# Pair products of a DLRM tower: two samples a product in 64-column strips of the PE array

## The reference

```python
e = jnp.stack([tbl_0[ids[:, 0]], ..., tbl_26[ids[:, 26]]], axis=1)   # [2048, 27, 128]
interactions = jnp.einsum('bfd,bgd->bfg', e, e)                     # a 27 x 27 gram per sample
x = interactions.reshape(B, 27 * 27)[:, TRIL_IDX]                   # 351 pairs
h = jnp.concatenate([bottom, x, bottom], axis=1)                    # 607 columns
h = jnp.maximum(h @ W_top1 + b_top1, 0.0)                           # 512
h = jnp.maximum(h @ W_top2 + b_top2, 0.0)                           # 256
y = h @ W_top3                                                      # 1
```

## Time and profile before

| | us |
|---|---|
| median of 3 runs | 420.68 |
| lowest, highest | 418.67, 421.84 |
| the profiled execution's own time | 419.41 |
| its span, first to last instruction | 417.6 |
| around the span | 1.8 |

### The profile page before, as it was taken

The page is one execution under the profiler, slowest core; times in us unless marked ns, Lnnn a source line. Parts: engine busy times, 40 slices in busy tenths (PEclk is TensorE's granted clock), DMA queues, the critical chain, the costliest instruction groups (busy, mean ns, idle before and its releaser), DMA issues.

```text
span 417.6 us, 8875 instructions
## 1 busy us (share of the span) xinstructions
PE 378.1 (91%) x3158; PEld 363.0 (87%) x3158; DVE 203.1 (49%) x493; ACT 157.4 (38%) x305; POOL 288.1 (69%) x279
## 2 busy tenths in 40 slices
PE   0457899959999989999899999999999999999987
PEld 0446789959999988999799998999999998999976
DVE  4587337924259124753349234744268235824140
ACT  2243342434332543235332453235423542335343
POOL 6777778777777778777777777777777777750000
PEclk9998999988999999999999999999999999999999
DMA  7999943557245661544324771645334652540000
GB/s 116 243 231 225 261 116 103 95 95 125 67 107 90 107 138 43 124 96 98 122 80 113 99 142 44 135 88 113 104 102 97 103 132 51 138 84 2 2 2 0
DMA packets 49790, 44.19 MB, mean 106 GB/s; under 512 B 30309, under 2 KB 42093, under 8 KB 49767
## 3 DMA queue, kind: packets, MB, share of 16 engines
q1 hardware_dynamic: 39440, 24.26, 30.9%
q0 software_dynamic: 8704, 17.84, 16.5%
q10 hardware_dynamic: 1623, 1.79, 1.6%
HBM read 39.01 MB, written 4.85 MB: 105 GB/s over the span
## 4 chain that ended last, share of the span: by engine, by line
PE 71%; DMA 12%; POOL 8%; issue 4%; ACT 3%; DVE 1%; SPq 1%; ACTq 0%; POOLq 0%
PE ps_build L742 26%; PE ps_gram L775 18%; PE ps_dense L783 8%; POOL rows L400 8%; DMA rows<-tbl_dram,idx 7%; PE ps_dense L811 6%; DMA raw<-tbl_dram 5%; PE ps_gram L771 3%; PE ps_build L754 2%; PE ps_dense L819 2%; PE ps_gram L754 2%; PE ps_gram L783 1%; ACT embT L561 1%; PE ps_build L811 1%; DVE table L415 1%
## 5 line engine op out<-in xcount | busy, mean ns | idle before, releaser
L400 POOL DMA_INDIRECT rows<-tbl_dram,idx x272 | 287.4, 1056 | 84.4 <-issue 77.4
L742 PE MATMUL ps_build<-hot,table 125*128 125x256 f32 x1280 | 164.2, 288 | 26.0 <-DVE table L415 18.4
L742 PEld LDWEIGHTS ps_build<-hot,table 125*128 125x128 f32 x1280 | 158.2, 194 | 26.8 <-issue 21.4
L440 DVE TENSOR_SCALAR hot<-id_raw 125x512 fp32r<-125x512 f32 x320 | 120.4, 435 | 5.5 <-PE ps_build L742 4.1
L775 PEld LDWEIGHTS ps_gram<-embT 128*107 128x107 f32 x896 | 89.8, 177 | 6.5 <-issue 3.0
L454 DVE COPY gram<-ps_gram 107x416 f32<-107x416 f32 x56 | 32.9, 588 | 125.0 <-PE ps_gram L775 120.6
L775 PE MATMUL ps_gram<-embT 128*107 128x104 f32 x896 | 92.4, 262 | 1.4 <-ACT embT L561 0.8
L554 ACT COPY embT<-ps_build 128x512 f32<-128x512 f32 x40 | 32.1, 804 | 108.6 <-PE ps_build L742 102.3
L573 ACT COPY gram<-ps_gram 107x416 f32<-107x416 f32 x56 | 28.4, 506 | 52.5 <-PE ps_gram L775 49.9
L783 PE MATMUL ps_dense<-pairT,w1p 120*128 120x256 f32 (+1 forms) x252 | 34.8, 283 | 0.0
L783 PEld LDWEIGHTS ps_dense<-pairT,w1p 120*128 120x128 f32 (+1 forms) x252 | 32.2, 191 | 0.0
(11 more groups left out here) (60 smaller groups left out, 169.4 us busy)
## 6 DMA issues: line engine op xcount, KB each, us to landing
id_raw<-ids_onehot_dram SPq DMA_DIRECT2D x40, 256.0 KB, 5.9
gram_dram<-gram SPq DMA_DIRECT2D x56, 84.5 KB
raw<-tbl_dram SPq DMA_DIRECT2D x10, 448.0 KB
rows<-tbl_dram,idx POOLq DMA_INDIRECT x272
bot<-bottom_dram SPq DMA_DIRECT2D x8, 128.0 KB, 6.5
w1p_raw<-w_pairs_dram ACTq DMA_DIRECT2D x1, 720.0 KB
raw<-tbl_dram SPq DMA_DIRECT2D x10, 52.0 KB
w2s<-w_dram ACTq DMA_DIRECT2D x1, 512.0 KB
```

The costliest lines, as they stand in the source:

```text
L400: nc.gpsimd.indirect_dma_start(rows[:, t, s * D:(s + 1) * D], None, tables[f], bass.IndirectOffsetOnAxis(idx[:, 2 * i + t, f:f + 1], 0)).t ...
L440: last = nc.vector.tensor_scalar(hot[0:VP, a % HOT_SLOTS, v, 0:w, :], shifted, float(v0 + v), None, ALU.is_equal)
L742: last = nc.tensor.matmul(bank[:, q * HALF:(q + 1) * HALF], table[0:VP, units[n][q], bits, row:row + D], hot[0:VP, a % HOT_SLOTS, v, q, :] ...
```

## The change

A product takes two samples (`DUO`): 53 stationary columns by 52 moving ones. Consecutive products go to one of two 64-column strips of the array (`tile_position`), and so to partitions 0 to 52 or 64 to 116 of PSUM. A tile is 64 products (128 pairs of instructions), 16 products to a bank, and the four gram banks hold the whole tile; each is emptied by one copy of 117 partitions × 416 elements, DVE's for banks 0 and 2 and ACT's for banks 1 and 3. `gram` holds both tiles. In the last half each sample is a product of its own, 26 × 26, in four 32-column strips: 128 products (256 pairs) a tile, two banks, one copy of 122 × 416 each. `embT` is no longer padded. The three `pairs_low` and `pairs_high` go before the gram copies of tile 0, `make_hot` of the next half goes three after tile 0 and two after tile 1, and layers 2 and 3 of the half before go behind all grams of tile 1.

```diff
-    GB = 8
-    GU = TILE // GROUP // GB
-    GRAMS = 2 * GU
-    GC = GROUP * PG
     JT = TILE // GROUP
-    GM = GROUP * FEATURES - 1
+    DUO = GROUP // 2
+    STRIP = DUO * PAD
+    GB = JT // 4
+    GRAMS = 4
+    GM = STRIP + DUO * FEATURES - 1
+    EB = JT // 2
...
-        gram = in_arena("gram", [GM, GROUP, PG, JT], fp32, 0)
+        gram = in_arena("gram", [GM, 2, DUO, PG, JT], fp32, 0)
...
+        def gram_piece(t, b):
+
+            src = gram_banks[b][0:GM, 0:GB * DUO * PG].rearrange("p (g c) -> p c g", g=GB)
+            return gram[:, t].rearrange("p k n j -> p (k n) j")[:, :, b * GB:(b + 1) * GB], src
+
+        def end_piece(t, b):
+
+            src = gram_banks[2 * t + b][0:GR, 0:EB * PG].rearrange("p (g n) -> p n g", n=PG)
+            return gram_end[:, :, t * JT + b * EB:t * JT + (b + 1) * EB], src
...
                 for k in range(GROUP):
-                    src = gram[k * FEATURES:k * FEATURES + PG, k, :, :].rearrange("p n j -> p (n j)")
+                    row = k // DUO * STRIP + k % DUO * FEATURES
+                    src = gram[row:row + PG, t, k % DUO, :, :].rearrange("p n j -> p (n j)")
...
-            def empty_gram(i, t, u):
-                if u == 0 and t == 0 and not is_half(i, FIRST):
+            def empty_gram(i, t):
+                if t == 0 and not is_half(i, FIRST):
                     dve.wait_ge(gram_out, TILE_OUT * 2 * i)
-                if u == 0 and t == 1 and not is_half(i, LAST):
-                    dve.wait_ge(gram_out, TILE_OUT * (2 * i + 1))
-                dve.wait_ge(grammed[1 if is_half(i, LAST) else 0], GRAMS * i + t * GU + u + 1)
                 if is_half(i, LAST):
-                    nc.vector.tensor_copy(*gram_pieces(t, u, 0))
-                    nc.vector.tensor_copy(*gram_pieces(t, u, 1)).then_inc(gram_dve, 1)
+                    dve.wait_ge(grammed[0], GRAMS * LAST + t + 1)
+                    nc.vector.tensor_copy(*end_piece(t, 0)).then_inc(gram_dve, 1)
                 else:
-                    nc.vector.tensor_copy(*gram_bank(u, 0)).then_inc(gram_dve, 1)
+                    for n in range(2):
+                        dve.wait_ge(grammed[0], GRAMS * i + 2 * t + n + 1)
+                        nc.vector.tensor_copy(*gram_piece(t, 2 * n + 0)).then_inc(gram_dve, 1)
...
-                for u in range(GU):
-                    empty_gram(i, 0, u)
-                    if u < 3:
-                        pairs_low(i - 1, u)
-                if more:
-                    make_hot(i + 1, 0)
-                for u in range(GU):
-                    empty_gram(i, 1, u)
-                    if more:
-                        make_hot(i + 1, 1 + u)
-
-            nc.vector.memset(emb_flat[:, HALF * FEATURES:HALF * PAD], 0.0).then_inc(pad_set, 1)
+                for c in range(3):
+                    pairs_low(i - 1, c)
+                grams(i, more)
+
+            def grams(i, more=True):
+                for t in range(2):
+                    empty_gram(i, t)
+                    for a in ((0, 1, 2), (3, 4))[t] if more else ():
+                        make_hot(i + 1, a)
...
             def second_tile(i, dense=None):
-                for u in range(GU):
-                    empty_gram(i, 1, u)
-                    if dense is not None and u < M2:
-                        layer2(dense, u)
-                    if dense is not None and u == M2:
-                        layer3(dense)
+                empty_gram(i, 1)
+                if dense is not None:
+                    for m in range(M2):
+                        layer2(dense, m)
+                    layer3(dense)
...
+            def pair_products(i, t):
+                pe.wait_ge(emb_done, BUILDS * i + nth("tile", t, TQ - 1) + 1)
+                for b in range(4):
+                    if t == 1 and b % 2 == 0:
+                        pe.wait_ge(gram_dve, GRAMS * i + b // 2 + 1)
+                    if t == 1 and b % 2 == 1:
+                        pe.wait_ge(gram_act, GRAMS * i + b // 2 + 1)
+                    for g in range(GB):
+                        for q in range(2):
+                            at = t * TILE + (b * GB + g) * GROUP + q * DUO
+                            x = embT[:, at:at + DUO, :]
+                            last = nc.tensor.matmul(
+                                gram_banks[b][STRIP * q:STRIP * q + GM - STRIP, g * DUO * PG:(g + 1) * DUO * PG],
+                                x.rearrange("p k g -> p (k g)")[:, 0:GM - STRIP], x[:, :, 1:FEATURES],
+                                start=True, stop=True, tile_position=(0, STRIP * q))
+                    last.then_inc(grammed[b % 2], 1)
+
+            def end_products(t):
+                pe.wait_ge(emb_done, BUILDS * LAST + nth("tile", t, TQ - 1) + 1)
                 for b in range(2):
...
+                    for g in range(EB):
+                        for k in range(GROUP):
+                            x = embT[:, t * TILE + (b * EB + g) * GROUP + k, :]
+                            last = nc.tensor.matmul(gram_banks[2 * t + b][PAD * k:PAD * k + PG, g * PG:(g + 1) * PG],
+                                                    x[:, 0:PG], x[:, 1:FEATURES], start=True, stop=True,
+                                                    tile_position=(0, PAD * k))
                     last.then_inc(grammed[b], 1)
...
             def relayout():
 
-                pe.wait_ge(gram_dve, GRAMS * HALVES)
-                pe.wait_ge(gram_act, GRAMS * HALVES)
+                pe.wait_ge(gram_dve, GRAMS * LAST + 2)
+                pe.wait_ge(gram_act, GRAMS * LAST + 2)
```

More of the change, by code:

```diff
@@ L506, in _ @@
                     split_table(q)
-            for n in range(GRAMS):
-                empty_gram(FIRST, n // GU, n % GU)
-                if n >= GRAMS - HOT_SLOTS:
-                    make_hot(1, n - GRAMS + HOT_SLOTS)
+            grams(FIRST)
             half(1)
@@ L626, in first_tile @@
             def first_tile(i, dense=None):
[L627 to L630 removed]
+                if dense is not None:
+                    for c in range(3):
+                        pairs_high(dense, c)
+                empty_gram(i, 0)
             def second_rows(i, dense=None):
@@ L879, in _ @@
             features(FIRST)
-            pe.wait_ge(pad_set, 1)
             first_tile(FIRST)
```

85 lines of the change are left out of this document (25 added, 60 removed).

## The result

The changed kernel takes 402.07 us (median of 4 runs, 401.51 to 407.32) where the kernel before took 421.26 in the same comparison (4 runs, 418.67 to 422.03): a ratio of 0.9583, 95% interval 0.9492 to 0.9673. The profiled execution took 401.51 (span 399.7) against 419.41 of the kernel before: 17.9 us less. I had forecast 413.6 and a range from 404, so the change did about two and a half times what I gave it. The direction holds, and so does the gain of PE with the gathers as the bound behind it; the size doesn't.

What follows compares the result with a forecast made beforehand. PE was taken as the bound, POOL's gathers close behind. Gain 7 us within the gathers' room, then last tile −0.7 + 0.2 and layer 3 +0.37: −7.1 from 419.41 gives 412.3; with the median 1.27 higher, 413.6, range 404 to 438.

Steps and rivals of the forecast that it cites:

- The grams: Gram products of halves 0 to 6: 31 ns a pair with strips side by side, a tile 4.0 us, saving 2.0.
- Borders: Switches between whole-array work and strips, twice a tile: 0.1 us each, 0.2 a tile.
- Layer 3: Layers 2 and 3 now adjacent: PE waits for ACT's relu and loses 0.37 us in each of seven halves.
- PE's half: PE's work in an ordinary half, 45.85 us before: two tiles save 2.0 each, less borders and the relu wait.
- The copies: Gram copies, 4 instead of 8 a half per engine at DVE 588 and ACT 506 ns: no time gained.
- The last half: Gram tiles of 256 small pairs at 24 ns, nearer to serial: 6.1 us a tile, saving 0.7.
- The relayout: After the last half's layers: its first bank waits for ACT to read layer 3's result, 0.8 us as before.
- The room ahead of PE: PE trails the gathered rows by some 10 us at the end; 7 taken as the gain before the last half's second tile.
- The step that failed: Gathers on POOL: pace held at 1.056 us plus about 0.30 issue, capping PE's gain at some 10 us.
- serial strips: Rival for the grams: strips take turns, an ordinary tile costs 0.6 us more, 428 us in all; chance 0.27.
- the fixed time a pair: Rival for the grams: below a fixed time fewer columns don't help; at 57 ns a pair 449 us; chance 0.21.
- late landings: Rival for the gathers: strips overlap but rows land 11 us late in every half, gain under 3 us, 418; chance 0.10.

Runs made afterwards that it cites:

- experiment 7: Separate kernel without the reference's computation: five phases of 34 gathers beside idle DVE, gram copies, one-hot parts, both in turn, subtractions; no whole time given.
- experiments 4 and 5: First: changed kernel unaltered on a slow chip, 628.61 us. Second: changed kernel, only tile 0's rows gathered anew after the first half, 486.55 us.

## Why the prediction was wrong

The steps in their order, own times of the profiled executions:

- **The grams.** I took 31 ns a pair between 26 and 57; it is 3.29/128 = 25.7, the end for strips fully side by side. By that line nothing is lost to the float32 product being two pairs in a row in one strip. A tile saves 2.7 us, not 2.0.
- **Borders.** I took 0.1 us each. The first part of layer 1 behind strips takes 1.63 instead of 1.46 us, layer 2 3.65 where two parts took 3.50: 0.15 to 0.17 on leaving the strips, nothing visible on entering them. Right in sum, 0.2 a tile.
- **Layer 3.** I took 0.37 us of waiting for the relu. From 113.91 to 115.07 it is 1.16 us where layer 3 took 0.95: 0.2.
- **PE's half**, from these, by forecast 45.85 − 4.0 + 0.4 + 0.37 = 42.6; measured 40.8 to 41.0.
- **The copies** cost what they did (587 and 507 ns, x28 each), and no copy is waited for in the grams. Right.
- **The last half.** I took 24 ns a pair, 6.1 us a tile. The bursts go at about 9 ns, so my "nearer to serial" was wrong, but PE stops on the way, so tile 0 takes 4.94 us (358.29 to 363.23) and tile 1 4.90. It gives 1.2 a tile more than forecast. Layer 2 behind it then takes 5.34 us instead of 3.65, in a stretch where the window shows a clock of 0.68:

```profile
375.05:380.38 5.33, 5.33 (x17) 4.09 (x18) 0.00 (x0) 0.98 (x2) 0.00 (x0) 0.68 0.01 3
```

  After the stop of 2.43 us and 0.4 us of work the lower clock level is granted for a part of that stretch (0.50 from 376 to 378 us), which costs 1.7 us of the 2.4 that the two tiles gave beyond the forecast.
- **The relayout** waits 0.78 us for ACT's `y`. Right, at 0.8.
- **The room ahead of PE.** Taken 7 of 10, measured 7.2. That the two agree is partly luck. I took the room to bind at the end, where PE then doesn't wait: its last wait for rows ends at 284.96, behind the last gather of that half. That gather ends at 273.86 instead of 281.73, 7.9 us earlier, and from there on PE runs at its own pace.
- **The step that failed** is the sentence "That is all that PE can gain before the last half's second tile, whatever its grams cost, unless POOL itself becomes faster", with a gather at 1.056 us in the sum, and with it "`make_hot` keeps its count, and DVE is half idle", where I cost its new place at nothing. I held POOL's pace fixed. Measured, 34 gathers take 44.5 us instead of 45.9, the last gather ends 10.6 us earlier, and the 272 gathers are busy 10.8 us less. Had it stayed where it was, the gain would be about 17.9 − 10.6 = 7.3 us, an estimate that moves everything behind it by the same amount; forecast were 7.1. It was foreseen in name only: the range leaves out "a faster POOL", and the sign that I gave for it was set too far away. A gather was to fall below 1.25 us with its issue; it fell from 1.35 to 1.31 only, and these 0.04 us, 238 times over, are 10 of the 10.6 us.

A faster gather could have been suspected from the trace of before. Its timeline in tile 1, with DVE's one-hot part beside it:

```profile
254.19 1.70 POOL L400 DMA_INDIRECT rows<-tbl_dram,idx  x1 [0.31 <-issue]
254.31 0.75 DVE L440 TENSOR_SCALAR hot<-id_raw 125x512 fp32r<-125x512 f32 x2
```

and the changed kernel at the same point:

```profile
246.05 0.75 DVE L430 TENSOR_SCALAR hot<-id_raw 125x512 fp32r<-125x512 f32 x2
246.11 1.21 POOL L390 DMA_INDIRECT rows<-tbl_dram,idx  x1 [0.30 <-issue]
```

The gather that starts 0.12 us ahead of the one-hot part (two instructions) takes 1.70 us; the one that starts 0.06 behind its start takes 1.21. A gather alone is 944 ns. Counted over the 238 gathers behind the first 34, the kernel before has 14 longer than 1.6 us, 13 of them over a one-hot part, nearly all in tile 1 right behind a gram copy, and one over a subtraction on the weights; the changed kernel has none. Eleven of the 14 are one and the same meeting: a one-hot part starts 0.12 to 0.18 us behind the gather, right behind a gram copy. Both profiles of the kernel before have eleven such meetings, and all 22 gathers take 1.69 to 1.74 us. Where a part starts that long behind a gather but not behind a gram copy, the gather takes 1.01 to 1.06. The changed kernel has one such meeting behind a copy, and that gather takes 1.03, so the moment and the copy aren't the whole condition. What these 238 take beyond 944 ns each is 23.9 us before and 13.7 after: 10.2 of the 10.8 us, and the 14 long ones alone hold 11.1. Shown is that one-hot parts delay a gather beside them and copies don't, and that the long gathers, over one-hot parts, are gone after the change. Not shown is which of the changes took them away, DVE's order or the pace of the grams that the parts follow: the phases of experiment 7 reproduce 1.09 to 1.33 us and not 1.70, and the edits of DVE's order ran only where POOL's pace doesn't count. The cause of the faster gathers is thus located and not proven.

Of the rivals, serial strips and the fixed time a pair are out at 25.7 ns (and about 9 ns for the smaller ones); late landings came true in part, with landings of 9.55 to 11.93 us, and are what the windows of 47.47 and 43.79 us hold.

## What to carry to other kernels

When a change frees time on the engine that bounds and a second engine is close behind, write down the second engine's pace as an estimate with its own range, and look for what disturbs it: the spread of one instruction's duration (0.94 to 1.70 us here) shows what could still be had. Put the sign of a moved pace as close as the sum is sensitive to it: here 0.04 us a gather were 10 us. Small independent products in different column strips, taken turn about, took 25.7 ns a pair here against 42 in one strip at a time; but count the instructions, since PE stopped after long runs of short ones, and longer products between them took most of that away. A gain read on one chip can have the other sign on the next (0.958 and 1.051 here), so time a change that multiplies instructions on several.

## What the runs showed of the hardware

- **Strips overlap although they share all rows.** 25.7 ns a pair turn about, 42 ns within one strip, about 9 ns in four strips of 26 columns. The Trainium skill (TensorE: Matmul & The Clock Gate, Part 3: Packing small matmuls — row/col tiling) says that a weight load overlaps matmuls in flight only if its row group differs; by that nothing would be gained, and the measurement decides against it. Its 2.38 times for three column strips lies beside 1.63 for two here.
- **PE stops in long runs of short products.** In the last half it stops for 1.54 and 2.43 us after 161 and 230 pairs, with nothing to wait for, and for 2.21 and 2.14 us in the kernel that gathers once. With longer products between, the stops fall from 4.6 to 1.2 us in all.
- **Gathers hold PE up on some chips**: 579 to 608 us against 419 to 422 for the same program. In the changed kernel PE has gaps of 0.5 to 1.2 us after four or five pairs while gathers run, and its granted clock is 0.805 instead of 0.957 (experiments 4 and 5).
- **DVE's kind of operation, and the moment of it, set a gather's duration**: 944 ns beside nothing or copies from PSUM, a median of 1087 beside comparisons from SBUF to SBUF, up to 1.74 us where one starts 0.12 to 0.18 us behind the gather, and once 26.14 us beside back-to-back subtractions of two SBUF operands. The Trainium skill (SBUF — State Buffer, Who interferes with whom) describes a port pair that DVE and GpSimd share as an exclusive lock, for DVE operations in a two-port mode or with two SBUF inputs. The trace agrees for the copies; for the comparisons it agrees if they run in such a mode, which no row here says. For an operation with two SBUF inputs the same section says that it contends with GpSimd instructions that read SBUF, and infers that it leaves the writing of a DMA's descriptors alone. Here it did stop a gather, which also reads its indices from SBUF; the trace doesn't tell which of the two was held.
